# Denominator sums of an attention kernel: four interleaved chains of key tiles against four consecutive groups, each merged when complete

## What is computed

```python
q = (x @ Wq.T).reshape(N, S, H, hd).transpose(0, 2, 1, 3)     # k and v likewise
energy = einsum('nhqd,nhkd->nhqk', q, k)
attn = softmax(energy / sqrt(hd), axis=3)
x = layernorm(x + einsum('nhql,nhld->nhqd', attn, v).transpose(0, 2, 1, 3).reshape(N, S, D))
w = (weights >= 0) * 2 - 1
x = layernorm(x + clip((x @ w.T) * scale + bias, -100, 100))
```

## Time and profile before

| | us |
|---|---|
| median of 3 runs (3016.4 to 3021.62) | 3019.92 |
| the profiled execution | 3020.84 |
| its span, first to last instruction | 3019.0 |
| PE busy | 2832.8 |
| ACT busy | 2344.3 |
| DVE busy | 2197.3 |
| POOL busy | 343.1 |

### The profile page before, as it was taken

One profiled execution on the slowest core, in us unless ns is written; L12 is line 12 of the kernel. 1 busy time (PEld: TensorE's weight loads), 2 busy tenths in 40 slices (PEclk: granted clock), 3 DMA queues, 4 the chain that ended last, 5 costly groups with the idle time before them and its releaser, 6 DMA issues.

```text
span 3019.0 us, 78291 instructions
## 1 busy us (share of the span) xinstructions
PE 2832.8 (94%) x29292; PEld 1429.3 (47%) x29292; DVE 2197.3 (73%) x1922; ACT 2344.3 (78%) x2902; POOL 343.1 (11%) x340
## 2 busy tenths in 40 slices
PE   8999999899999999999989999899999999997998
PEld 7888888633333333333333333333333333335887
DVE  4433334378878787788778778777877877786998
ACT  3333333399989889898989999898998989894665
POOL 0000000010000000000000000000000000003665
PEclk9999999999999999999999999999999999998999
DMA  5454454447566655756566575656657565654563
GB/s 199 167 186 176 167 183 178 169 108 158 114 147 136 146 134 129 156 114 147 129 143 136 124 167 114 143 122 152 139 124 154 118 152 112 153 113 142 204 207 126
DMA packets 223344, 444.15 MB, mean 147 GB/s; under 512 B 15410, under 2 KB 130098, under 8 KB 198836
## 3 DMA queue, kind: packets, MB, share of 16 engines
q0 software_dynamic: 27216, 198.19, 32.8%
q1 hardware_dynamic: 186596, 224.71, 23.3%
q10 hardware_dynamic: 9216, 16.78, 1.5%
HBM read 123.47 MB, written 117.96 MB: 80 GB/s over the span
## 4 chain that ended last, share of the span: by engine, by line
PE 40%; DMA 14%; issue 11%; ACT 8%; DVE 7%; POOL 1%; ACTq 0%; DVEq 0%; POOLq 0%; SPq 0%
PE banks L633 15%; PE banks L662 15%; DMA sums<-sums 14%; ACT probs L770 7%; PE banks L998 6%; DVE sums L821 6%; PE banks L678 2%; PE banks L987 1%; PE banks L980 1%; DVE sums L817 1%; PE banks L994 0%; ACT wf_scaled L750 0%; POOL sums L601 0%; POOL score_rows L583 0%; PE banks L981 0%
## 5 line engine op out<-in xcount | busy, mean ns | idle before, releaser
L770 ACT ACTIVATE probs<-banks 128x1024 f32<-128x1024 f32 x2048 | 1908.0, 1172 | 91.0 <-PE banks L633 81.5
L633 PE MATMUL banks<-score_rows 97*32 97x512 f16 x16384 | 1227.6, 385 | 70.2 <-ACT probs L770 29.2
L662 PE MATMUL banks<-probs,v_keys 128*32 128x512 f32 x8192 | 1162.6, 597 | 16.8 <-issue 15.4
L821 DVE TENSOR_TENSOR sums<-sums,probs 128x2048 f32<-128x2048 f32 x512 | 1134.4, 2282 | 23.9 <-ACT probs L770 23.7
L633 PEld LDWEIGHTS banks<-score_rows 97*32 97x32 f16 x16384 | 438.7, 96 | 1043.5 <-ACT probs L770 572.9
L817 DVE TENSOR_TENSOR sums<-probs 128x2048 f32<-128x2048 f32 x256 | 569.4, 2286 | 396.7 <-ACT probs L770 396.7
L662 PEld LDWEIGHTS banks<-probs,v_keys 128*32 128x32 f32 x8192 | 295.2, 112 | 241.4 <-issue 64.2
L345 DVE TENSOR_TENSOR qk_lo<-banks,qk_hi 128x512 f16<-128x512 f32 x128 | 88.5, 691 | 239.3 <-ACT qk_hi L289 239.3
L289 ACT ACTIVATE qk_hi<-banks 128x512 f16<-128x512 f32 x128 | 76.4, 597 | 232.6 <-PE banks L243 232.6
L243 PE MATMUL banks<-xT_hi,w_hi 128*128 128x512 f32 x512 | 201.2, 393 | 1.5 <-DVE xT_lo L321 1.5
L243 PE MATMUL banks<-xT_hi,w_lo 128*128 128x512 f32 x512 | 199.3, 389 | 0.0
(11 more groups left out here) (92 smaller groups left out, 2157.8 us busy)
## 6 DMA issues: line engine op xcount, KB each, us to landing
sums<-sums POOLq DMA_DIRECT2D x189, 1024.0 KB, 8.5
x_in<-in_L_attn_x SPq DMA_DIRECT2D x17, 1024.0 KB, 7.1
scratch_q_raw<-qk_raw SPq DMA_DIRECT2D x16, 1024.0 KB, 5.5
scratch_k_raw<-qk_raw SPq DMA_DIRECT2D x16, 1024.0 KB, 5.6
scratch_v<-v_out SPq DMA_DIRECT2D x16, 1024.0 KB, 5.0
score_rows<-scratch_q_hi SPq DMA_DIRECT2D x128, 128.0 KB, 3.0
score_rows<-scratch_k_hi SPq DMA_DIRECT2D x128, 128.0 KB, 2.9
v_keys<-scratch_v SPq DMA_DIRECT2D x64, 256.0 KB, 6.5
```

The lines of the kernel that those rows point to most:

```text
L633: last = nc.tensor.matmul(scores_of(unit)[part, i, :], k_rows[:, h, keys], q_rows[:, h, qb * BLK:(qb + 1) * BLK], start=True, stop=True)
L662: last = nc.tensor.matmul(banks[rows, out_bank(qb), :], v_keys[:, kt, rows], probs[:, kt % P_RING, h, :], start=(kt == 0), stop=(kt == KT ...
L770: nc.scalar.activation(probs[:, kt % P_RING, heads, :], scores_of(qb * UNITS + u), ACT.Exp, scale=SCALE / GAIN ** 2).then_inc(a_prob, 1)
L821: nc.vector.tensor_tensor(total, total, probs[:, kt % P_RING], ALU.add).then_inc(a_sum, 1)
```

## The change

The four partial sums now cover consecutive tiles: 0 to 3, 4 to 7, 8 to 11 and 12 to 15 (`GROUPS`, `PER`). The first group is summed in `total` (two of them, for even and odd blocks), the others each in a `partial` of its own, of which there is one set. A group takes three adds: the first adds its first two tiles, and each of the others needs the one before it. POOL merges a group into `total` as soon as its adds are done, by one DMA, and waits for that DMA before it turns to the next; behind each landing it raises `a_merged`, for which PE waits before the denominators and DVE before it writes a `partial` again. The denominators move from tile 12 to tile 10 of the next block, and with them PE's loop border and ACT's copy. In the last block the second and third group are merged, and the fourth goes to PE by itself: two parts instead of four. Apart from this, the projection stage ends with waits that count the credit, so that the last block's stores have landed too.

```diff
-CHAINS = 4
+GROUPS = 4
+PER = KT // GROUPS
-DEN_TILE = 12
+DEN_TILE = 10
...
-        sp.wait_ge(s_qst, 48 * NBLK)
-        sp.wait_ge(s_kst, 48 * NBLK)
-        sp.wait_ge(s_vst, 16 * NBLK)
+        sp.wait_ge(s_qst, 48 * NBLK + 48)
+        sp.wait_ge(s_kst, 48 * NBLK + 48)
+        sp.wait_ge(s_vst, 16 * NBLK + 16)
...
-    sums = sb("sums", [P, 2, CHAINS, G, BLK], FP32)
+    total = sb("total", [P, 2, G, BLK], FP32)
+    partial = sb("partial", [P, GROUPS - 1, G, BLK], FP32)
...
-        def merge(it, qb):
+        def merge(it, qb, groups):
             st = it * QB + qb
-            pool.wait_ge(a_sum, (st + 1) * KT + P_RING)
-            pool.sem_inc(a_order, 1)
-            pool.dma_start(sums[:, qb % 2, 0], sums[:, qb % 2, 1], accum_op=ALU.add).then_inc(a_half, 16)
-            pool.dma_start(sums[:, qb % 2, 2], sums[:, qb % 2, 3], accum_op=ALU.add).then_inc(a_half, 16)
-            pool.wait_ge(a_half, st * 32 + 32)
-            pool.sem_inc(a_order, 1)
-            pool.dma_start(sums[:, qb % 2, 0], sums[:, qb % 2, 2], accum_op=ALU.add).then_inc(a_merge, 16)
+            for g in groups:
+                pool.wait_ge(a_sum, st * KT + PER * (g + 1) + P_RING)
+                pool.sem_inc(a_order, 1)
+                pool.dma_start(total[:, qb % 2], partial[:, g - 1], accum_op=ALU.add).then_inc(a_merge, 16)
+                pool.wait_ge(a_merge, (st * (GROUPS - 1) + g) * 16)
+                pool.sem_inc(a_merged, 1)
         with pool.Fori(0, LAST) as it:
             for qb in range(QB):
-                merge(it, qb)
-        for qb in range(QB - 1):
-            merge(LAST, qb)
+                merge(it, qb, range(1, GROUPS))
+        for qb in range(QB):
+            merge(LAST, qb, range(1, GROUPS if qb < QB - 1 else GROUPS - 1))
...
+        pe.sem_inc(a_merged, GROUPS - 1)
...
         def denominators(it, qb):
             st = it * QB + qb
+            parts = [total[:, qb % 2]]
             if it is LAST and qb == QB - 1:
+                pe.wait_ge(a_merged, (st + 2) * (GROUPS - 1) - 1)
                 pe.wait_ge(a_sum, (st + 1) * KT + P_RING)
-                chains = CHAINS
+                parts.append(partial[:, GROUPS - 2])
             else:
-                pe.wait_ge(a_merge, st * 16 + 16)
-                chains = 1
+                pe.wait_ge(a_merged, (st + 2) * (GROUPS - 1))
             pe.wait_ge(a_out, st + 1)
-            for chain in range(chains):
+            for part in parts:
                 for h in range(G):
                     rows = slice(HD * h, HD * h + HD)
-                    last = nc.tensor.matmul(banks[rows, out_bank(qb), :], ones[:], sums[:, qb % 2, chain, h, :],
-                                            start=(chain == 0), stop=(chain == chains - 1))
+                    last = nc.tensor.matmul(banks[rows, out_bank(qb), :], ones[:], part[:, h, :],
+                                            start=(part is parts[0]), stop=(part is parts[-1]))
...
-                for kt in range(CHAINS, KT):
-                    total = sums[:, qb % 2, kt % CHAINS]
+                for kt in range(KT):
+                    g, place = divmod(kt, PER)
+                    if place == 0:
+                        continue
+                    into = total[:, qb % 2] if g == 0 else partial[:, g - 1]
                     dve.wait_ge(a_prob, st * UNITS + 2 * kt + 2 + SLOTS)
-                    if kt < 2 * CHAINS:
-                        dve.wait_ge(a_den, st + 1)
-                        freed = 1 if kt < 2 * CHAINS - 1 else CHAINS + 1
-                        nc.vector.tensor_tensor(total, probs[:, kt - CHAINS], probs[:, kt], ALU.add).then_inc(a_sum, freed)
+                    if place == 1:
+                        if g == 0:
+                            dve.wait_ge(a_den, st + 1)
+                        else:
+                            dve.wait_ge(a_merged, st * (GROUPS - 1) + g)
+                        nc.vector.tensor_tensor(into, probs[:, (kt - 1) % P_RING], probs[:, kt % P_RING], ALU.add).then_inc(a_sum, 2)
                     else:
-                        dve.wait_ge(a_sum, st * KT + (kt - CHAINS + 1 if kt >= 3 * CHAINS - 1 else kt - 2 * CHAINS + 1) + P_RING)
-                        nc.vector.tensor_tensor(total, total, probs[:, kt % P_RING], ALU.add).then_inc(a_sum, 1)
+                        dve.wait_ge(a_sum, st * KT + kt + P_RING)
+                        nc.vector.tensor_tensor(into, into, probs[:, kt % P_RING], ALU.add).then_inc(a_sum, 1)
```

More of the change, by code:

```diff
@@ L415, in attend @@
     a_order = sem("a_order")
-    a_half = sem("a_half")
     a_merge = sem("a_merge")
+    a_merged = sem("a_merged")
     a_den = sem("a_den")
```

## The result

The kernel after the change takes 3059.5 us in the median of four runs (3049.9 to 3066.5), against 3019.2 before: ratio 1.0132, 95% interval 1.0097 to 1.0166. It is slower by 40 us, where 2928 was forecast. The profiled execution took 3049.9 us.

What follows compares the result with a forecast made beforehand. ACT was taken as the attention stage's bound, idle only 162 us. Gains of 70 (denominator waits), 14 (stall aftermath), 6 (block starts) and 3 (end) sum to 93 us: 3020.8 - 93 = 2928, range 2885 to 2970.

Steps and rivals of the forecast that it cites:

- Branches on PE and ACT stay: Attention stage: the loop branches of both engines were to remain as they were, with no gain or loss counted.
- The wait and its 70 us: ACT's waits before the denominators' copy (line 755) were to go, 70.1 us, as the last merge lands in time.
- Adds: DVE: dependent adds 2.32 us apart, last ending E+3.4; 27.4 us a block, hidden under ACT's 30.0.
- The merges: POOL: three of 1 MB one after another, 7.7 us each alone, last landing E+13.3; at 10.2 us each, E+20.8.
- The rule by which adds on DVE might hold back POOL's issues: Shared SBUF access: up to 2.3 us before each issue, last landing near E+20, sum unchanged; the trace showed no such wait.
- The end and the stores: Last block: 16 denominator records instead of 32, 2.7 us, gain 3; projection store waits cost nothing, at most 5.0 us once.
- The clock: A sign of being right: granted clock 1.00 in the attention stage.
- partly given back: Rival, 0.17: merges fill queues beside loads and PE's code, other ACT stalls grow by half; some 40 us return, 2968.
- More than the wait: Rival, 0.10: stalls before exponentials come from two merges side by side and go too, 40 us more: 2888.
- The slower case: Rival, 0.06: POOL's chain of merges becomes the bound, slower above 10.4 us a merge; at 11 us, 3135.

Runs made afterwards that it cites:

- run 2: Kernel before plus one accumulating 1 MB copy per item, issued some 3 us ahead of PE's jump: 3099.8 us, 1.0271.
- run 3: Kernel after, last block's third-group merge held until ACT passes its border: 2990.7 us; also denominators at tile 8, first block's second-group merge held for PE: 2954.5.
- run 7: Kernel after, merges in four by partitions: 3455.8 us; same on three-items-a-pass kernel: 3489.7; by head: 2936.3. Kernel before, ACT-queue copy at three later places: 3026.9, 3049.9, 3052.9.
- run 4: Kernel before with parts of the change: merge pair one after the other, 3099.9 us; new store waits alone, 3017.3; denominators at tile 13, 3051.2.
- Run 5: Kernel after with denominators at tile 7 and PE's and ACT's loops taking three items a pass: 2911.4 us, 0.9647.
- run 1: Kernel after with denominators and PE's loop border at another tile: tile 12, 2973.7 us; tile 7, 2949.5 us.
- run 6: Kernel before plus a plain 1 MB copy per item: ACT's queue, 3022.8 us; POOL's queue, 3017.2; POOL's one key tile later, 3081.9.

## Why the prediction was wrong, point by point

**The step that failed** is half a sentence: "Branches on PE and ACT stay". I had costed them at nothing because their number and code didn't change, and had not laid the new times of the merges over the places of the jumps, though the times stood in my working. With E the end of a block's exponentials, the third group's merge was to be issued at E-2.7 and to land at E+5.0, and ACT's border is at E; the second group's was to be in flight from E-11.0 to E-3.3, and PE's new border, at E+22.8 with a block of 30.0, is at E-7.2 of the block that it stands in. The runs showed 3.0 us more in each of PE's 14 jumps and 4.2 in 11 of ACT's, 88 us of waiting, and more than that in time (run 2). Forecast and result are 131 us apart. Taking the hold from ACT's border gave back 69 of them (run 3), cutting the merges by head some 120 (run 7); the 50 or so between are by subtraction PE's, whose jumps are then still 0.6 us longer than before.

**The wait and its 70 us: right.** No row is left of it, and a block's last merge lands at E+13.0 in second blocks (forecast E+13.3), at E+16.1 in fourth ones (measured medians; E+19.1 was the latest of all), ahead of E+22.8.

**Adds: right.** The dependent ones start 2.33 us apart (2.32 forecast), the last ends at E+3.5 (E+3.4). The merges: 7.0, 8.0 and 10.3 us (7.7 and 10.2 taken). The rule by which adds on DVE might hold back POOL's issues did not show: an issue takes 0.86 us in the median and 1.02 at most, as before.

**The end and the stores: right.** PE ran dry for 3.10 us and needed 3.61 for 16 records (2.7 forecast), 6.7 in all, against 3.81 + 5.33 = 9.1: 2.4 us of the 3. The store waits by themselves moved nothing.

**The clock: wrong.** I had named 1.00 in the stage; it is 0.96: behind the new stalls of 5 us it falls (0.56 above) as it did behind the old ones. With the merges cut by head it is 0.99.

**The case "partly given back"** named the code and the shared engines, at 2968 and 0.17. It had the resource and not the mechanism: I let short stalls grow by half, where the jumps themselves wait for a whole transfer. **"More than the wait"** was true in kind: part of the stalls behind pairs of merges went (run 4). What it is worth no run shows by itself. Run 5 lies under the forecast, but some 37 us of that come from fewer borders, a term that neither the forecast nor this case had; without them the fastest kernels here, 2936 and 2949, lie above 2928.

**The slower case** was the wrong one for this kernel: merges took 8.0 us, not 10.4. With pieces of 32 partitions, 12.3 us a merge, it came true as described: PE waited 287 us on POOL's merges.

## What to carry to other kernels

Where an engine's loop jumps back, look which transfers are in flight there: a jump needs its code, and the code waits for the large transfer that it meets. Move the transfer (run 3), cut it so that every piece still spans all partitions (run 7, and not by partitions), or unroll the loop so that there are fewer borders (run 5). And when a change moves a DMA, write its new times beside every place that needs another DMA, code included, and not only beside the instructions that use its data.

## What the runs showed of the hardware that was not expected

- Code packets wait for a megabyte in flight on either kind of queue: PE's start 7.0 to 7.2 us after the issue of an accumulating one (5.9 once, in run 3; ACT's 5.6 to 7.7) and 3.9 to 4.9 after a plain one, about half a microsecond ahead of its landing where no loads run beside it. With four pieces of 256 KB by head queued they start ahead of the first piece's landing in eight held jumps of ten. The Trainium skill ("DMA: Bandwidth & Descriptors", Queues, rings and completion order) says that a DMA engine goes round its queues and changes only when a whole packet of one is drained; and The descriptor swizzle there gives an engine's share of 1 MiB as eight data descriptors, few enough for one such packet (a packet there is a run of descriptors, not one record of the trace). Read together they fit what the trace shows of whole transfers and of pieces by head, where a 1 MB transfer was one turn and a piece was mostly one. They don't account for the pieces by partitions, where ACT's code waited for the last of four in 12 jumps.
- The Trainium skill ("Runtime: NRT & Kernel Launch", Instruction fetch mechanics) says that a taken branch out of the loaded window must fetch its target first. The trace agrees, and adds the price here: 3.3 to 3.9 us on PE with one packet inside, 4.7 to 5.2 with two, 2.5 to 3.1 on ACT, with nothing in the way.
- A transfer issued up to 0.55 us ahead of a jump didn't hold its code back, one issued 0.9 us or more ahead did (runs 1, 6 and 7).
- The same megabyte accumulated in pieces of 32 partitions took 12.3 us in the median, in pieces of 2 KB from all 128 9.2, in one piece 8.0.

Left open: why pieces of 32 partitions are slow, why code waits for the last of them, and whether run 5 with merges cut by head would be faster still; it wasn't run.
